# Moving layer 0's first-half norms into attention, its shared experts behind the first half's logits, and scatter waits to pairs

## What is computed

```python
x = x + _layernorm(_L0_attn_ref(_layernorm(x), ...))   # 16 heads, comparison masks instead of a softmax
x = x + _layernorm(_L0_ffn_ref(_layernorm(x), ...))    # 32 experts, top 4, and a shared expert of width 512
x = x + _layernorm(_L1_attn_ref(_layernorm(x), ...))   # an RWKV block
x = x + _layernorm(_L1_ffn_ref(_layernorm(x), ...))    # 8 experts, top 2, and a shared expert of width 512
```

```python
logits = flat @ router_w.T + router_bias
scores = softmax(logits);  topk_scores, topk_idx = top_k(scores, 4)
topk_scores = topk_scores / clip(topk_scores.sum(-1), 1e-12)
h = silu(einsum('nd,ehd->neh', flat, gate_w)) * einsum('nd,ehd->neh', flat, up_w)
expert_out = einsum('neh,edh->ned', h, down_w)
out = (take(expert_out, topk_idx) * topk_scores).sum(1)
out = out + silu(flat @ sgate_w.T) * (flat @ sup_w.T) @ sdown_w.T
```

## Time and profile before

| | |
|---|---|
| median of 3 runs | 1191.71 us (1190.69 to 1194.6) |
| profiled execution | 1191.5 us, of which the profile's span is 1189.7 us |
| PE busy | 877.6 us (74%) |
| DVE busy | 763.5 us (64%) |
| ACT busy | 658.0 us (55%) |
| POOL busy | 504.0 us (42%) |

### The profile page before, as it was taken

How to read it: one execution, slowest core, us unless ns; L and a number is a source line. 1 busy time by engine, 2 the same in 40 slices (tenths; PEclk the granted TensorE clock), 3 DMA queues, 4 the chain that set the end, 5 groups by cost and what they waited for, 6 DMA issues and landing times. The chain is left out here.

```text
span 1189.7 us, 19661 instructions
## 1 busy us (share of the span) xinstructions
PE 877.6 (74%) x5732; PEld 702.6 (59%) x5732; DVE 763.5 (64%) x2389; ACT 658.0 (55%) x1352; POOL 504.0 (42%) x634
## 2 busy tenths in 40 slices
PE   3796666666146999997995367777668989999910
PEld 2633455555135888996993134444456979999910
DVE  5479578887765466222676799998868541115636
ACT  4354777777554224664664676777775645555500
POOL 0002555555216666666774773000005564035154
PEclk9998677777556999998997677788877999999965
DMA  7960000000601115647763110000031133233132
GB/s 204 290 191 1 1 0 0 0 0 1 240 20 46 48 52 169 199 147 197 200 170 90 46 45 25 1 0 1 1 141 50 55 97 95 63 83 92 41 98 62
DMA packets 133841, 96.98 MB, mean 82 GB/s; under 512 B 11648, under 2 KB 125696, under 8 KB 132736
## 3 DMA queue, kind: packets, MB, share of 16 engines
q1 hardware_dynamic: 121472, 70.79, 20.0%
q0 software_dynamic: 12288, 25.19, 7.4%
HBM read 45.61 MB, written 50.33 MB: 81 GB/s over the span
## 5 line engine op out<-in xcount | busy, mean ns | idle before, releaser
L1122 POOL DMA_INDIRECT e_xs<-h_tok,rows_of x128 | 127.8, 998 | 96.1 <-DVEq L1614 35.3
L735 ACT ACTIVATE mask<-ps_q,k_neg 128x256 bf16<-128x256 f32 x256 | 100.7, 488 | 35.0 <-PE ps_q L850 35.0
L1135 POOL DMA_INDIRECT e_got<-e_ys,e_rows_of x64 | 61.8, 966 | 118.3 <-DMA e_ys<-e_y_rows 88.6
L850 PE MATMUL ps_q<-q_parts,pick 128*128 (+1 forms) x256 | 59.2, 366 | 49.7 <-DVE mask L651 42.1
L1270 PE MATMUL e_ps_gu<-e_w_all,e_x_turned 128*128 x384 | 92.0, 383 | 0.5 <-ACT e_x_turned L1453 0.5
L1777 DVE TENSOR_TENSOR e_hidden<-e_ps_gu,e_hidden 128x512 f32<-128x512 f32 x48 | 33.2, 691 | 87.5 <-ACT e_hidden L1460 87.2
L1465 ACT ACTIVATE e_hidden<-e_ps_up 128x512 f32<-128x512 f32 x80 | 47.8, 597 | 72.1 <-PE e_ps_up L1308 71.8
L1122 POOL DMA_INDIRECT e_xs<-h_tok,e_rows_of x64 | 63.9, 998 | 50.6 <-DVEq L1614 24.0
L2282 POOL DMA_INDIRECT c_got<-e_ys,rows_of x64 | 70.3, 1098 | 33.3 <-issue 19.2
L1325 PE MATMUL e_ps_y<-e_w_all,e_h_turned 128*128 x640 | 84.2, 275 | 0.0
L651 DVE TENSOR_TENSOR mask<-ps_q,k_tok 128x1024 bf16<-128x1024 f32 x64 | 75.2, 1216 | 10.2 <-PE ps_q L850 8.2
(11 more groups left out here) (410 smaller groups left out, 2604.2 us busy)
## 6 DMA issues: line engine op xcount, KB each, us to landing
e_x_rows<-e_xs SPq DMA_DIRECT2D x68, 256.0 KB, 2.9
e_ys<-e_y_rows SPq DMA_DIRECT2D x68, 256.0 KB, 2.5
e_xs<-zeros SPq DMA_DIRECT2D x2, 6144.0 KB, 34.2
e_w_all<-in_w SPq DMA_DIRECT2D x4, 1536.0 KB, 13.0
e_xs<-zeros SPq DMA_DIRECT2D x2, 2560.0 KB, 27.4
e_w_all<-in_w SPq DMA_DIRECT2D x4, 1024.0 KB, 10.7
x_tok<-in_x SPq DMA_DIRECT2D x4, 512.0 KB, 6.2
e_xs<-h_tok,rows_of POOLq DMA_INDIRECT x128, 2.2
```

The lines of the kernel that those rows point to most:

```text
L735: last = nc.scalar.activation(mask[u][QS // 2 + j][keys][:, h * T:(h + 1) * T], psq[1][:, h * T:(h + 1) * T], ACT.Sign, bias=k_neg[u][:, k ...
L850: last = nc.tensor.matmul(psq[0 if on_dve else 1][:, h * T:(h + 1) * T], pick[:, (quad * HQ + h) * P:(quad * HQ + h + 1) * P], q_parts[:, ...
L1122: nc.gpsimd.indirect_dma_start(out=xs[part], out_offset=bass.IndirectOffsetOnAxis(ap=rows_of[:, t * K + k:t * K + k + 1], axis=0), in_=til ...
L1135: nc.gpsimd.indirect_dma_start(out=got[t % GB][:, k * P:(k + 1) * P], out_offset=None, in_=ys[part], in_offset=bass.IndirectOffsetOnAxis(a ...
```

## The change

All of it lies in attention's last block and in `routed`.

- DVE's and POOL's loops over batches keep the first half rolled and write the second half out (`rolled_first_half`). In steps 9, 11 to 14 and 15 DVE does pieces of a generator `front` at four places of the step: the root chain for the first 16 tiles' `y`, the statistics of the summed rows, and the root chain for these. POOL normalizes and adds a group of the first half at the end of each of steps 10 to 13 (`front_sums`), and in the step behind the last batch, ahead of the last numerators, writes the first half's `h_tok` (`front_norms`).
- The routed block of layer 0 therefore begins with the statistics of the second half alone, and PE turns groups 0 to 3 at once. The second half's norms, sums and splits are spread over the shared units, which follow `totals(0)` and `ranks(0)`; the second half's turns stand behind units 4, 6, 9 and 11, its routes two units later. `ps_sum` is one bank instead of two.
- The scatters count on three semaphores, one for every third pair; behind each pair POOL waits for the landing of the pair before. This holds for both layers. Eight more semaphores are made ready at the start.

```diff
+def rolled_first_half(eng, n, step):
+
+    assert n % 4 == 0
+    step(0, 0)
+    with eng.Fori(0, n // 4) as i2:
+        step(i2 * 2 + 1, 1)
+        step(i2 * 2 + 2, 0)
+    for i in range(n // 2 + 1, n + 1):
+        step(i, i % 2)
 ...
+                    cf, cs = Chain(dve, front_own), Chain(dve, front_stats)
+
+                    def front_root(rstd_, shift_, done):
+                        yield from env["merge_steps"](cf, stats[:, 0:HT * 6], mean, rstd_, spread, P // 2)
+                        cf.mark(nc.vector.tensor_scalar(spread, rstd_, 1.0 / P, LN_EPS, ALU.mult, ALU.add))
+                        yield
+                        cf.wait()
+                        yield from env["inverse_root_steps"](cf, rstd_, spread, root_tmp)
+                        nc.vector.scalar_tensor_tensor(shift_, mean, -1.0, rstd_, ALU.mult, ALU.mult).then_inc(done, 1)
+                        yield
+
+                    def front():
+
+                        dve.wait_ge(stats_done, FROM + HT)
+                        yield from front_root(scale_y, shift_y, front_scaled)
+                        for g in range(GROUPS // 2):
+                            dve.wait_ge(front_added, FROM + g + 1)
+                            for t in range(g * TPG, (g + 1) * TPG):
+                                cs.mark(nc.vector.bn_stats(stats[:, t * 6:t * 6 + 6], x_tok[:, t * P:(t + 1) * P]))
+                                yield
+                        cs.wait()
+                        yield from front_root(rstd, shift_x, front_ready)
+
+                    early = front()
+                    pieces = {NB // 2 + 1: 4, NB // 2 + 3: 1, NB // 2 + 4: 1, NB // 2 + 5: 1, NB // 2 + 6: 1, NB // 2 + 7: 4}
+
+                    def advance(b_):
+                        for _ in range(pieces.get(b_, 0) if isinstance(b_, int) else 0):
+                            next(early, None)
+
                     def step(b_, parity):
                         now, before = not is_at(b_, NB), not is_at(b_, 0)
                         if now:
                             masks(b_, parity, 0)
+                        advance(b_)
                         if before:
                             sums_in(b_ - 1)
+                        advance(b_)
                         if now:
                             masks(b_, parity, 1)
+                        advance(b_)
                         if before:
                             results(b_ - 1)
                         else:
                             constant_parts()
-                    pipelined(dve, NB, step)
+                        advance(b_)
+                        if is_at(b_, NB - 1):
+                            for _ in early:
+                                pass
+                    rolled_first_half(dve, NB, step)
 ...
+                    def front_sums(g):
+                        if g == 0:
+                            pool.wait_ge(front_scaled, FROM + 1)
+                        for t in range(g * TPG, (g + 1) * TPG):
+                            y = y_tok[:, t * P:(t + 1) * P]
+                            nc.gpsimd.tensor_scalar(y, y, scale_y[:, t:t + 1], shift_y[:, t:t + 1], ALU.mult,
+                                                    ALU.add).then_inc(front_rows, 1)
+                        pool.wait_ge(front_rows, FROM + (g + 1) * TPG)
+                        x = x_tok[:, g * GW:(g + 1) * GW]
+                        nc.gpsimd.tensor_tensor(x, x, y_tok[:, g * GW:(g + 1) * GW], ALU.add).then_inc(front_added, 1)
+
+                    def front_norms():
+                        pool.wait_ge(front_ready, FROM + 1)
+                        for t in range(HT):
+                            nc.gpsimd.tensor_scalar(h_tok[:, t * P:(t + 1) * P], x_tok[:, t * P:(t + 1) * P],
+                                                    rstd[:, t:t + 1], shift_x[:, t:t + 1], ALU.mult,
+                                                    ALU.add).then_inc(front_normed, 1)
+
                     def step(b_, parity):
 ...
+                        if not now:
+                            front_norms()
 ...
+                        if isinstance(b_, int) and NB // 2 + 2 <= b_ < NB // 2 + 2 + GROUPS // 2:
+                            front_sums(b_ - NB // 2 - 2)
+                    rolled_first_half(pool, NB, step)
+                    pool.wait_ge(front_normed, FROM + HT)
 ...
-    TURN_AT = (9, 12, 15, 18)
-    AT_TOTALS, AT_RANKS, AT_OWNERS = (17, 19, 22) if gated else (23, 26, 29)
+    TURN_AT = (4, 6, 9, 11) if gated else (9, 12, 15, 18)
+    AT_TOTALS, AT_RANKS, AT_OWNERS = (20, 22, 24) if gated else (23, 26, 29)
 ...
+        scale_y, shift_y, shift_x = env["scale_y1"], env["shift_y1"], env["shift_x1"]
+        ADDED, SCALED, NORMED = GPP, 2, GPP if gated else 2
 ...
+            ps_t, ps_l, ps_count, ps_sum = ring[0], ring[1], ring[2], ring[3:]
 ...
+                        last = (part + 1) * PT * K // 2 - 1
+                        for pair in range(last - 2, last + 1):
+                            sp.wait_ge(scattered[pair % 3], 32 * (pair // 3 + 1))
 ...
+                def pair_landed(pair):
+                    if pair >= 0:
+                        pool.wait_ge(scattered[pair % 3], 32 * (pair // 3 + 1))
 ...
-                                in_=tile(h_tok, t), in_offset=None).then_inc(scattered[t // TPG], 16)
-                        if (t + 1) * K % 8 == 0:
-                            pool.wait_ge(scattered[t // TPG], 16 * K * (t % TPG + 1))
+                                in_=tile(h_tok, t), in_offset=None).then_inc(
+                                    scattered[(t * K + k) // 2 % 3], 16)
+                            if k % 2:
+                                pair_landed((t * K + k) // 2 - 1)
 ...
-                    turn(GPP)
-                    turn(GPP + 1)
-                    totals(0)
-                    ranks(0)
-                    owners(0)
-                    for g in range(GPP, GROUPS):
-                        if g >= GPP + 2:
-                            turn(g)
-                        route(g)
-                else:
-                    totals(0)
-                    unit(0)
-                    ranks(0)
-                    unit(1)
-                    owners(0)
-                for n in range(0 if gated else 2, SU):
+                totals(0)
+                unit(0)
+                ranks(0)
+                unit(1)
+                owners(0)
+                for n in range(2, SU):
                     unit(n)
-                    if not gated and n in TURN_AT:
+                    if n in TURN_AT:
                         turn(GPP + TURN_AT.index(n))
-                    if not gated and n - 2 in TURN_AT:
+                    if n - 2 in TURN_AT:
 ...
+                    for g in range(GPP):
+                        turned(g)
+                        if g < 2:
+                            norm_y(GPP + g)
+                        else:
+                            high(g - 2)
+                    norm_x(GPP)
+                    norm_x(GPP + 1)
+                    norm_y(GPP + 2)
+                    exps(0)
+                    for n in range(SU):
+                        shared(n)
+                        if n == 0:
+                            norm_y(GPP + 3)
+                        if n in (1, 2):
+                            high(n + 1)
+                        if n in (6, 7):
+                            norm_x(GPP + n - 4)
+                        if n in TURN_AT:
+                            turned(GPP + TURN_AT.index(n))
+                            high(GPP + TURN_AT.index(n))
+                        if n == 21:
+                            exps(1)
                 else:
                     norm_x(2)
 ...
-                    together(adds(0, 1))
-                    together(x_scales(0), adds(2, 3))
-                    together(x_scales(1), adds(4, 5))
+                    together(adds(4, 5))
 ...
-                if not gated:
-                    split(0)
+                split(0)
                 dve.wait_ge(constants, FROM + 7)
                 bases(0)
                 place(0)
-                table(0)
 ...
-                        if n % SH == BEHIND and n > SH:
+                        if n % SH == 1 and n > SH:
                             shared_out(n // SH - 1)
-                        if n < 16:
+                        if n == 0:
+                            table(0)
+                            split(1)
+                        if n == 1:
+                            together(adds(6))
+                        if n == 2:
+                            together(adds(7))
+                        if n == 3:
+                            together(x_scales(3))
+                        if n in (4, 6):
+                            split(n // 2)
+                        if n == 7:
+                            shares(0)
+                        if n - 2 in TURN_AT:
+                            split(GPP + TURN_AT.index(n - 2))
```

(30 more changed lines are left out.)

39 lines of the change are left out of this document (7 added, 32 removed).

## The result

The changed kernel takes 1173.16 us (median of 4 runs, 1170.51 to 1176.06) where the kernel before took 1193.13 (median of 4); the ratio is 0.983 (95% interval 0.9808 to 0.9852). The forecast was 1168, in a range of 1157 to 1183. The profiled execution took 1174.4, its span is 1172.3, which is 17.4 less than before.

| stage | before | after | difference | forecast |
|---|---|---|---|---|
| to attention's end | 304.95 | 317.15 | +12.2 | +7.6 |
| routed block of layer 0 | 332.27 | 299.40 | -32.9 | -31.0 |
| RWKV block | 242.07 | 244.73 | +2.7 | 0 |
| layer 1's feed-forward to the end | 310.4 | 311.0 | +0.6 | 0 |

A forecast was written before the change was run, and what follows sets the result against it. PE, busy with the shared experts, was taken to set run 0's start, by 5.9 us over the data. From 1191.5, -31.0 behind attention, +7.3 in attention and +0.3 for semaphores gave 1168.1, say 1168; range 1157 to 1183.

The forecast's parts named there:

- step 1: Front of the block behind attention: logits come 14.75 us earlier, and the scatter starts at 335.8.
- Step 2: Scatter of part 0: pair waits leave no stop, so rows are ready for PE at 423.6.
- Rival C: Scatter: the pair waits only move the stops, 9.6 us a part; 1181 us in all; chance 0.07.
- Step 3: Shared experts: PE is free at 418.8, before the data, so run 0 starts 29.2 us earlier.
- Rival B: Shared experts: DVE's additions stop PE by 10 us, not 1.5, so PE is later than the data; 1173; chance 0.11.
- restart price: Start of run 0: the gap of 4.8 us slows PE's turns and first products, +1.3 us.
- Step 4: Between the runs: the load follows run 0's last store and PE waits 4.0 us instead of 7.07, -3.1.
- Step 5, L: Attention's lengthening by the early work put on DVE and POOL: 7.3 us, bounds 3.5 and 12.
- X: Time of one POOL tensor_scalar in the early norms and sums, taken as 0.33 us.
- rival A: Attention gives more back: X is 0.53 and attention lengthens by 32X - 2.1 = 14.9 us; 1176; chance 0.16.
- D: Attention: rival A's mechanism with X above 1.04 makes the kernel slower, 1192 us there, 1206 at 1.5; chance 0.08.
- Step 6: The rest: layer 1's scatter waits bring 0, eight more semaphores at the start cost 0.3 us.

The follow-up runs named there:

- run 0: Not a follow-up kernel: the first of PE's two stretches of routed expert work in layer 0; in the kernel before it began at 452.84 and ended at 537.9 us.
- before_pairs: The kernel before with the scatters' pair waits alone added, in both layers: 1190.31 us, ratio 0.9970 to the kernel before.
- run 1: Not a follow-up kernel: the second of PE's two stretches of routed expert work in layer 0; in the kernel before it began at 544.98 us.
- order_only: The changed kernel without the early front and with the old scatter stops, leaving only the new order behind attention: 1193.08 us, ratio 0.9990 to the kernel before.
- no_front: The changed kernel with the first half's norms, sums and roots back at the routed block's start: 1177.13 us, ratio 0.9870 to the kernel before.

## Why the prediction was right, and where it was off

*The bound and step 1.* That PE's order set run 0 in the kernel before was right (before_pairs). Logits came 13.3 behind attention's end, 14.5 by the hand count; the first scatter 29.5 for 30.9.

*Step 2.* 84.0 from the first scatter to SP's load for 84.9; two pairs in flight leave no stop in the usual case. Rival C is out by 15 us.

*Step 3.* PE was free 114.4 behind attention's end (forecast 113.9), the rows there at 116.4 (118.7). The balance is finer than forecast, 2 instead of 4.8, and it tips to PE without the early front. Rival B is out. The restart price of 1.3 was too high: run 0 took 85.5, 0.4 more than before.

*Step 4.* The gap was forecast at 4.0 and is 4.21. From the first turn of run 1 to the block's end it took 93.2 instead of 92.2, which the forecast put at nothing; over the other kernels it is 92.9 to 94.3, and the cause is not shown.

*Step 5, L.* This step failed in size: 11.9 measured in the first profile (12.2 less 0.3 for the semaphores) for 7.3, at the upper bound of 12. Its parts, from the starts of DVE's sums: first root 1.4 (1.5 forecast), second root 1.3 (1.0), last norms 3.6 (2.1), and the five steps with statistics and POOL's sums 5.5 (1.2 + 1.5). So two terms were mis-sized. The norms: X is 0.433 (6.93 for 16), not 0.33; the row nearest in shape, the copy, was the wrong neighbour. POOL's sums: their length was taken as 2.7 and is 3.2 (1.91 for four scalars, 1.28 for the wide sum), and the forecast let a batch be late by 0.8 in half of the cases, while each of the four came 1.0 to 1.7 later than a batch of the same kind before, statistics counted in. The row showed a slack of 1.36 ahead of ACT's masks, and a POOL step that is 3.2 longer ate that in every batch (four waits of 3.3 for the columns). That is rival A's mechanism, and its formula 32X - 2.1 gives 11.8 with the X measured; only A's X of 0.53 was too high, and with it its 1176. The time fell between the two, 5 above the forecast (from medians of 1193.13 and 1173.16 the gain is 20.0, where the forecast had 23 below 1191.5). In the profiles attention is 4.6 above its forecast, the block behind it 1.9 below, and the stages behind that 3.3 above (2.7 of it the RWKV block's longer length). That the first two misses have opposite signs is luck. D, the same mechanism with X above 1.04, is out by the 0.433.

The Trainium skill (GPSIMD Engine Reference, Engine selection) says that an elementwise operation of one input runs at roughly line rate on POOL. Here the tensor_scalar of 128x128 took 0.433 where POOL's copy of that shape takes 0.29, so the measurement decides against reading X off that rule.

*Step 6.* Layer 1's part is 0.6 longer in the profile, within what repeats show; the semaphores' 0.3 are there (the first sums start at 146.81, at 146.50 before).

*The arithmetic.* Two small slips changed nothing: four times half of 1.1 + 1.8 is 5.8, not 5.6, and 16 x 0.33 lies 1.9 above the 3.4 that rival A leaves for the norms, where step 5 has 2.1.

## What to carry to other kernels

Count the value of an edit together with the bound that it uncovers: the new order alone was worth 0 and the pair waits alone 2, but both together 15 (order_only, before_pairs, no_front). Work put on an engine that idles in a loop was nearly free only where that engine waits in any case: the same four POOL steps of 3.2 us lengthened attention by 5.5 ahead of what ACT needed and by 1.5 inside POOL's own wait (DVE's statistics counted in both, and moved too), and with the norms shared out and the root chains spread the whole early front cost 1.3. Where an operation is in no row, let the rival with the dearer price and the tighter slack have more weight.

## What the hardware showed unexpectedly

Two further waits in a stop of POOL made it 2.03 instead of 1.53, 0.25 each. A POOL operation of two inputs of 128x512 took 1.27 in attention and 1.60 where it met DVE's additions of two SBUF tiles (1.67 in the earlier trace rows), and two such DVE additions then took 0.91 and 1.12 instead of 0.69. In the timeline of POOL and DVE after the change, the one that began later was the longer each time:

```profile
322.67 0.61 POOL L1186 CAST e_sgate_hi<-e_x_rows 128x512 fp32r<-128x512 f32 x1 [4.09 <-DMA e_x_rows<-in_sup]
322.92 0.91 DVE L1580 TENSOR_TENSOR x_tok<-x_tok,y_tok 128x512 f32<-128x512 f32 x1 [1.77 <-ACT y_tok L1437]
323.37 1.60 POOL L1188 TENSOR_TENSOR e_sgate_lo<-e_x_rows,e_sgate_hi 128x512 fp32r<-128x512 f32 x1
...
324.90 0.61 POOL L1186 CAST e_sup_hi<-e_x_rows 128x512 fp32r<-128x512 f32 x1
324.94 1.12 DVE L1580 TENSOR_TENSOR x_tok<-x_tok,y_tok 128x512 f32<-128x512 f32 x1 [0.20 <-ACT y_tok L1437]
```

The casts came first and took 0.61. In the earlier trace rows the addition came first, by 0.14, and took its 0.69, and POOL's difference took 1.67. So the 2.4 times that the prediction read from these rows has such a meeting in it; 1.27 for 0.69 is 1.8 times. The Trainium skill (SBUF — State Buffer, Who interferes with whom) has a DVE operation with two SBUF inputs contend with what POOL reads; these numbers agree.
